# Adjacency product and top-2 expert network: low parts written over their block in a ring of eight, rows pitched at 4096 B, weight copies three blocks ahead in the last stage

## The reference

```
h   = item_feat @ W_item.T + b_item                      # 10000 x 128
b   = layernorm(x) @ W_user.T + b_user                   # 10000 x 128
x1  = x + relu(adj @ h + b)                              # adj: 10000 x 10000
xf  = layernorm(x1)
p   = softmax(xf @ gate_w + gate_b)                      # 8 experts
cw  = the two largest p of each row, 0 elsewhere
out = x1 + sum over e of cw[:, e] * (gelu(xf @ W1[e] + b1[e]) @ W2[e] + b2[e])
```

## Time and profile before

| | us |
|---|---|
| median of three runs | 1902.14 |
| lowest, highest | 1897.42, 1909.39 |
| the profiled execution | 1902.33 |
| its span in the profile | 1900.5 |
| TensorE matmuls busy | 1489.7 (78%) |
| VectorE busy | 1297.4 (68%) |
| ScalarE busy | 1058.1 (56%) |
| POOL busy | 812.8 (43%) |

### The profile page before, as it was taken

The page is one execution under the profiler, slowest core; times in us unless marked ns, Lnnn a source line. Parts: engine busy times, 40 slices in busy tenths (PEclk is TensorE's granted clock), DMA queues, the critical chain, the costliest instruction groups (busy, mean ns, idle before and its releaser), DMA issues. The chain is left out here.

```text
span 1900.5 us, 23348 instructions
## 1 busy us (share of the span) xinstructions
PE 1489.7 (78%) x6505; PEld 1194.9 (63%) x6505; DVE 1297.4 (68%) x2462; ACT 1058.1 (56%) x1227; POOL 812.8 (43%) x507
## 2 busy tenths in 40 slices
PE   7998998998988979898898898988989863233221
PEld 6876776776766767677676776766767652222221
DVE  6887887887877878777787787877878753222110
ACT  5766665666665666667666676666766632122120
POOL 2012221231627355273552744626437255555555
PEclk9999998999999999899999999999989876677675
DMA  9988998998989888898998999989989834222222
GB/s 342 322 299 299 314 313 297 314 319 282 289 277 288 255 279 283 265 296 267 290 298 277 290 283 277 291 279 288 283 274 301 261 91 98 30 32 33 29 27 18
DMA packets 226519, 458.52 MB, mean 241 GB/s; under 512 B 78409, under 2 KB 113334, under 8 KB 226332
## 3 DMA queue, kind: packets, MB, share of 16 engines
q1 hardware_dynamic: 123942, 425.69, 67.2%
q0 software_dynamic: 92144, 27.11, 9.8%
q10 hardware_dynamic: 10390, 5.25, 0.9%
HBM read 429.03 MB, written 31.13 MB: 242 GB/s over the span
## 5 line engine op out<-in xcount | busy, mean ns | idle before, releaser
L676 DVE TENSOR_TENSOR a_lo<-raw,a_hi 128x1000 fp32r<-128x1000 f32 (+1 forms) x800 | 935.5, 1191 | 256.1 <-ACT a_hi L534 245.2
L534 ACT ACTIVATE a_hi<-raw 128x1000 fp32r<-128x1000 f32 (+1 forms) x800 | 814.6, 1029 | 444.0 <-DMA raw<-in_adj_main 328.2
L943 PE MATMUL acc<-a_hi,h_hi 128*128 128x500 f32 x1580 | 669.2, 424 | 126.2 <-DVE a_lo L676 98.2
L944 PE MATMUL acc<-a_lo,h_hi 128*128 128x500 f32 x1580 | 634.4, 402 | 0.0
L945 PE MATMUL acc<-a_hi,h_lo 128*128 128x500 f32 x1580 | 634.0, 401 | 0.0
L473 POOL DMA_INDIRECT out<-yr_sb,tok_at x156 | 356.5, 2285 | 417.8 <-DVE yr_sb L846 372.6
L943 PEld LDWEIGHTS acc<-a_hi,h_hi 128*128 128x128 f32 x1580 | 309.9, 196 | 239.9 <-DVE a_lo L676 168.1
L945 PEld LDWEIGHTS acc<-a_hi,h_lo 128*128 128x128 f32 x1580 | 309.3, 196 | 65.8
L944 PEld LDWEIGHTS acc<-a_lo,h_hi 128*128 128x128 f32 x1580 | 310.5, 197 | 56.7 <-issue 4.6
L453 POOL DMA_INDIRECT lists<-rows_sb,dest_at x160 | 239.4, 1496 | 145.9 <-DVE dest_at L797 73.2
L440 POOL TENSOR_TENSOR rstd_sb<-var_sb,power_sb 125x4 f32<-125x4 f32 x20 | 38.2, 1910 | 308.7 <-DVE var_sb L699 308.7
(11 more groups left out here) (160 smaller groups left out, 1320.5 us busy)
## 6 DMA issues: line engine op xcount, KB each, us to landing
raw<-in_adj_main SPq DMA_DIRECT2D x780, 500.0 KB
xg_sb<-lists SPq DMA_DIRECT2D x39, 273.4 KB
xr_sb<-in_xR SPq DMA_DIRECT2D x20, 250.0 KB
out<-x_sb ACTq DMA_DIRECT2D x20, 250.0 KB
items<-in_itemT SPq DMA_DIRECT2D x13, 384.0 KB, 6.5
lists<-rows_sb,dest_at POOLq DMA_INDIRECT x160
out<-yr_sb,tok_at POOLq DMA_INDIRECT x156
lists<-in_filling SPq DMA_DIRECT2D x8, 273.4 KB
```

Of the source, the lines that this page charges most:

```text
L534: nc.scalar.activation(a_hi[q][0:rows, 0:cols], raw[s][0:rows, 0:cols], ACT.Copy).then_inc(hi_ready, 1)
L676: nc.vector.tensor_tensor(a_lo[q][0:rows, 0:cols], raw[s][0:rows, 0:cols], val(a_hi[q][0:rows, 0:cols]), ALU.subtract).then_inc(lo_ready, 1)
L943: nc.tensor.matmul(acc[:, 0:T], w_hi, m_hi, start=(k == 0), stop=False)
L944: nc.tensor.matmul(acc[:, 0:T], w_hi, m_lo, start=False, stop=False)
```

## The change

Three things change.

1. The ring. `raw` has eight buffers. The tensors `a_lo` are now eight as well and are allocated at the addresses of `raw` (the `with` closes before they are allocated), so VectorE's subtraction writes the low part over the block from which it is made. Four separate `a_lo` buffers and, counted together, 4,000 B of SBUF per partition go (13 buffers of 4,000 B become 12). The slot of position p is free for position p + 8 when TensorE has used it, so SyncE's wait goes from `lo_ready` with p - 5 to `adj_used` with p - 8. `a_hi` still has four buffers.
2. The rows of an adjacency block lie 4096 B apart in DRAM instead of 4000 B; the 96 B behind each row are zero and aren't loaded.
3. In the last stage POOL copies the weights of block n + 3 ahead of the additions of block n, instead of n + 2. `tok_at`, `w_block` (two buffers) and the lists of the other engines stay.

```diff
-RAW = 5
+
+LINE = 1024
+RAW = 8
@@ buffers
-        raw = [sb(f"raw{s}", [P, CT * T]) for s in range(RAW)]
+
+        with ExitStack() as whole:
+            raw = [whole.enter_context(nc.sbuf_tensor(f"raw{s}", [P, CT * T], fp32)) for s in range(RAW)]
+        a_lo = [sb(f"a_lo{s}", [P, CT * T], fp32r) for s in range(RAW)]
         a_hi = [sb(f"a_hi{s}", [P, CT * T], fp32r) for s in range(SPL)]
-        a_lo = [sb(f"a_lo{s}", [P, CT * T], fp32r) for s in range(SPL)]
@@ the second set of work buffers
-                 dict(rows=raw[0], hi=a_hi[0][:, 0:T], lo=a_lo[0][:, 0:T], g=halves(raw[1]),
-                      g_hi=halves(a_hi[1]), g_lo=halves(a_lo[1]), y=raw[2], yr=raw[3])]
+                 dict(rows=raw[0], hi=a_hi[0][:, 0:T], lo=a_lo[4][:, 0:T], g=halves(raw[1]),
+                      g_hi=halves(a_hi[1]), g_lo=halves(a_lo[5]), y=raw[2], yr=raw[3])]
@@ SyncE, load_step
-                    sp.wait_ge(lo_ready, i * NPOS + (p - RAW + 1))
+                    sp.wait_ge(adj_used, i * NPOS + (p - RAW + 1))
                 if p < NC:
-                    sp.dma_start(raw[s][:, :], adj_main[i, p]).then_inc(raw_landed[s], 16)
+                    sp.dma_start(raw[s][:, :], adj_main[i, p, :, 0:CT * T]).then_inc(raw_landed[s], 16)
@@ POOL, last stage
             weights(NLATE + 1)
+            weights(NLATE + 2)
             for n in range(NLATE, BLOCKS):
-                if n + 2 < BLOCKS:
-                    weights(n + 2)
+                if n + 3 < BLOCKS:
+                    weights(n + 3)
                 add(n, NB)
@@ VectorE, split_lo
-                nc.vector.tensor_tensor(a_lo[q][0:rows, 0:cols], raw[s][0:rows, 0:cols],
+                nc.vector.tensor_tensor(a_lo[s][0:rows, 0:cols], raw[s][0:rows, 0:cols],
@@ TensorE, adj_step
-                    m_lo = a_lo[q][:, c * T:(c + 1) * T]
+                    m_lo = a_lo[p % RAW][:, c * T:(c + 1) * T]
@@ layout of the input
+    adj_main = _np.zeros((NB, NC, P, LINE), _np.float32)
+    adj_main[:, :, :, 0:CT * T] = blocks[:, :, :KT * P].reshape(NB, T, NC, CT, P).transpose(0, 2, 4, 3, 1).reshape(NB, NC, P, CT * T)
```

More of the change, by code:

```diff
@@ L1104 @@
     blocks = adj.reshape(NB, T, N)
+    adj_main = _np.zeros((NB, NC, P, LINE), _np.float32)
+    adj_main[:, :, :, 0:CT * T] = blocks[:, :, :KT * P].reshape(NB, T, NC, CT, P).transpose(0, 2, 4, 3, 1).reshape(NB, NC, P, CT * T)
     arrays = {
-        "adj_main": blocks[:, :, :KT * P].reshape(NB, T, NC, CT, P).transpose(0, 2, 4, 3, 1).reshape(NB, NC, P, CT * T),
+        "adj_main": adj_main,
         "adj_rem": blocks[:, :, KT * P:].transpose(0, 2, 1),
```

## The result

The changed kernel takes 1807.19 us (three runs, 1804.49 to 1810.38), before 1902.14: a ratio of 0.9497 with a 95% interval of 0.9443 to 0.9552. 1819 was forecast, in a range of 1752 to 1873. The profiled execution took 1804.49 us, its span is 1802.7.

A forecast was written before the change was run, and what follows sets the result against it. DMA engines and TensorE were taken as close to full in the passes, a chain of waits as setting the last stage. 1902.3 - 31.8 (end) - 52 (ring) = 1818.5, say 1819 us, range 1752 to 1873.

The forecast's parts named there:

- The end: Last stage: weight copies ahead of the additions let TensorE's work run beside them; -31.8 us.
- The period of 14.96 us: Last stage, blocks 30 to 43: time between first additions, 6.93 + 5.02 + 3.01, with the token-slot wait still on the path.
- The bound of 12.72: Last stage: period in us of all 16 blocks if the token-slot wait didn't count, 65 us less.
- Rival (c): Last stage: the token-slot wait is hidden and the end falls by 65 us, to 1785; chance 0.08.
- The ring: Passes after pass 0: eight slots let late loads be issued 4 us or more earlier; -52 us.
- 3.0 us a pass, 14 x 3.0 = 42, and 2.0 in the five early passes: Ring's gain: 42 us in the passes with expert blocks, 10 in the early ones, whose lateness was called smaller.
- Their 8.5 us: Most a pass with blocks can win: 5.0 us of idling behind late low parts, some 3.5 of half-speed clock.
- The pitch: Adjacency rows at 4096 B: value nil; bounds -9.7 to +7.8 us of DMA time a pass.
- Rival (b): Passes: aligned rows run at the best window's 161 ns throughout; 122 us less, with the end 1748; chance 0.14.
- Writing in place: VectorE's low part written over its own input: nil, from two small instructions of 420 and 419 ns.
- Rival (a): Passes: stream bound by bandwidth and SyncE's stops, deeper ring gives nothing, only the end gains: 1871 us; chance 0.2.
- Rival (d): Passes: slots come free too late, a load has 4.3 us instead of 7.6; slower, 1992 us; chance 0.06.

The follow-up runs named there:

- e1: Kernel before with only POOL's weight copies of the last stage three blocks ahead: ratio 0.985, last stage 327.8 us.
- e5: Changed kernel with eight token slots, six of them for the last 17 blocks: 1771.6 us, ratio 0.935.
- e6: Changed kernel with POOL's power for the tail's layernorm ahead of the additions of the block before, in the passes: 1786.9 us, ratio 0.944.
- e12: Kernel of e9 with the gelu of a pass's first block two positions later, and the steps that hang on it moved: 1734.1 us, ratio 0.912.
- e9: Changed kernel with the edits of e5 and e6, and SyncE's gathers and load of x three positions later: ratio 0.929.
- e3: Kernel before with the rows at 4096 B and nothing else: ratio 1.002.
- e4: Changed kernel with the last stage's weight copies two blocks ahead again: ratio 0.972.
- e2: Changed kernel with rows at 4000 B and the old list of the last stage, so the ring alone against the kernel before: ratio 0.971.
- e8: Changed kernel with a ring of five slots in place of eight, slots still freed by TensorE: 2077.8 us, ratio 1.097.

## Why the prediction was right

- **The end.** Right in mechanism and size: -31.8 forecast, -34.3 measured in the stage, -35.5 by e1. The period of 14.96 us was read from three rows of the old trace; 14.89 came out. The rest of the 2.5 us: one old period of 17.19 us stood for all 13, whose mean was 17.46 because one of them took 20.47. The bound of 12.72 was right for the case that the token slot doesn't bind, as e5 shows (12.71). That up, down and the transposes run beside the additions held: those of blocks 35, 34 and 33 run from 1582.17 to 1587.68, around the start of the additions of block 32 at 1584.20, though up itself waits for the low part that stands behind the token slot. Rival (c), a hidden wait for the token slot, is refuted by the row with 11.06 us of wait for the additions and by e5, where the wait is gone and the period falls.
- **The ring.** Right in sign and sum, -52 against -63.5, wrong in its division. The term mis-sized is "3.0 us a pass, 14 x 3.0 = 42, and 2.0 in the five early passes". The early passes gave 6.0 each, 3.8 of idle time and 2.2 of busy time at a higher clock. I had called their lateness smaller, for which no row stood, and taken a smaller gain than in the later ones, though no expert blocks were there to take it back. The later ones gave 2.2. Their 8.5 us were counted as idle time behind late low parts, 5.0, and clock. 2.6 of the 5.0 did go, but 2.5 came back in the wait for the power on POOL; what was gained there is mostly busy time, 1.4 us a pass. The earlier trace rows did not hold the row of that wait, and I had not asked which waits other than the late one would grow when the engines arrive earlier. Behind it lay others, the stream's lateness again (e6) and ScalarE's pause at position 16; without that pause the clock went from 0.96 to 0.99 (e12 against e9). The two wrong sizes were of opposite sign, 20 us too little in the early passes and 11 too much in the later ones, so that the sum came out near is in part luck.
- **The pitch.** Nil, as forecast; e3 and e4 show it. Rival (b), aligned rows at the rate of the best window, falls.
- **Writing in place.** L681 takes 1185 ns, L676 took 1191: nil.
- **Rival (a)**, a ring that gives nothing, falls with e2. **Rival (d)** is a true mechanism (e8) that eight slots outweigh.
- **What SyncE's stops cost.** I named them as what is left behind the ring. They did grow. e9 removes most of them without a measurable gain, but brings a wait of TensorE for the gathered rows of 1.3 us a pass, so their price stays open.

## What to carry to other kernels

A buffer ring has a price and a depth: count from landing to release, and what remains of depth times cadence is the time a load has. An in-place ring lengthens the hold and pays only if the depth grows by more (here the kernel with five slots and the late release was 9.7% slower than before, and eight slots alone gained 2.9%). When all engines get to a point earlier, look in their lists for what does not get earlier; a wait that was small before takes the gain, and one behind it takes that in turn. Ahead of a change in one engine's order, follow the next semaphore on the slowest chain, down to a slot of 16 B.

## What the runs showed of the hardware

- TensorE's clock counts beside its waits: 1345 instructions took 311.95 us at a mean granted clock of 0.95 and 300.87 at 0.99, 11.1 us of the 30.0 that the early passes gained. After an idle time of 4.48 us the granted clock was 0.50 (494.0 to 495.6 us), the level of 1.2 GHz, and the matmuls behind it took 0.77 and 0.62 us instead of 0.39.
- Rows of 4000 B at a pitch of 4000 B were loaded at up to 410 GB/s; a pitch of 4096 B changed neither the time of a pass nor the whole by a measurable amount, in either ring (e3; e4 against e2).
- Accumulating additions of 125 rows of 512 B were started 2.3 us apart; the next block's, which wait for them to land, began 5.8 us after the last had begun (e5), and that is 5.8 of the 12.7 us that were left of a block.
